# Graph attention with experts: POOL waits for the landing of its gathers in every second step

## What is computed

```python
alpha = a_src[src] + a_dst[dst]                     # leaky relu, exp(alpha - shift), then
out   = segment_sum(h[src] * coef[:, :, None], dst) # one sum per target node
```

```python
e = leaky_relu(a_src[src] + a_dst[dst]); msg = h[src] * alpha[:, :, None]
agg = segment_sum(msg, dst); scores -> top 2 of 4 -> softmax -> g
out = sum over e of g[..., e] * (gelu(x @ W1[e] + b1[e]) @ W2[e] + b2[e])
```

## Time and profile before

| | |
|---|---|
| median of the timed runs | 4169.92 us |
| profiled execution: span | 5269.4 us |
| first edge stage in it (143 to 3084 us) | 2941 us, 420 steps |
| second edge stage in it (3229 to 5126 us) | 1897 us, 265 steps |
| POOL busy | 2649.1 us, 50% of the span |
| DVE busy | 3039.4 us, 58% |
| PE busy | 3476.8 us, 66% |

### The profile page before, as it was taken

How to read it: one execution, slowest core, us unless ns; L and a number is a source line. 1 busy time by engine, 2 the same in 40 slices (tenths; PEclk the granted TensorE clock), 3 DMA queues, 4 the chain that set the end, 5 groups by cost and what they waited for, 6 DMA issues and landing times. The chain is left out here.

```text
span 5269.4 us, 87248 instructions
## 1 busy us (share of the span) xinstructions
PE 3476.8 (66%) x16727; PEld 2890.9 (55%) x16728; DVE 3039.4 (58%) x9074; ACT 1492.7 (28%) x4965; POOL 2649.1 (50%) x2767
## 2 busy tenths in 40 slices
PE   5555555665566665666655537888888888888860
PEld 4444444444454444444444436777777777777760
DVE  5566655555565666666666665555555555555558
ACT  3222222222222222222222213333333333333310
POOL 1555555555555555555555522555555555555540
PEclk9777777777777777777777766888888888888865
DMA  5322333332333333333332242111111111111118
GB/s 121 82 78 75 84 82 81 84 84 79 82 82 99 101 101 102 100 101 101 101 84 78 77 79 49 20 20 22 20 20 22 20 20 22 20 21 21 20 16 239
DMA packets 224394, 356.43 MB, mean 68 GB/s; under 512 B 65743, under 2 KB 143761, under 8 KB 224051
## 3 DMA queue, kind: packets, MB, share of 16 engines
q0 software_dynamic: 114560, 234.67, 19.2%
q1 hardware_dynamic: 100624, 109.13, 7.5%
q10 hardware_dynamic: 8867, 9.05, 0.6%
HBM read 294.17 MB, written 45.66 MB: 64 GB/s over the span
## 5 line engine op out<-in xcount | busy, mean ns | idle before, releaser
L791 POOL DMA_INDIRECT msg<-table,idx x1680 | 1630.7, 971 | 1305.1 <-ACT rel L806 844.6
L1466 POOL DMA_INDIRECT xmsg<-xtable,xidx x1060 | 1002.8, 946 | 889.0 <-ACT xidx L1482 589.7
L1159 PE MATMUL psS_e<-msg,hot 128*125 128x260 f32 x3360 | 1182.9, 513 | 281.4 <-issue 162.2
L1159 PEld LDWEIGHTS psS_e<-msg,hot 128*125 128x125 f32 x3360 | 815.5, 254 | 512.3 <-issue 337.3
L888 DVE TENSOR_TENSOR room<-room,psS_e 125x260 f32 x842 | 356.5, 423 | 361.7 <-remote 180.9
L1024 DVE TENSOR_TENSOR msg<-msg,psW_e 128x1024 f32<-128x1024 f32 x420 | 509.5, 1213 | 8.8 <-issue 1.1
L812 ACT CAST hotT<-psT_e 125x512 bf16<-125x512 f32 x422 | 244.7, 580 | 951.6 <-remote 649.7
L1012 DVE TENSOR_REDUCE look<-psD_e 128x32 f32<-128x96 f32 x420 | 106.6, 254 | 700.7 <-remote 553.8
L1076 PE MATMUL psD_e<-ad_b,hotT 125*128 x1684 | 133.9, 182 | 559.8 <-issue 151.3
L1655 PE MATMUL psY<-w,hid 128*125 128x256 f32 x1600 | 457.1, 447 | 56.7 <-issue 29.6
L1065 PEld LDWEIGHTS psT_e<-ident,hot 128*125 128x125 f32 x1692 | 320.7, 240 | 248.2 <-ACT hotT L812 157.7
(11 more groups left out here) (308 smaller groups left out, 4436.9 us busy)
## 6 DMA issues: line engine op xcount, KB each, us to landing
msg<-table,idx POOLq DMA_INDIRECT x1680
experts_out<-y_room SPq DMA_DIRECT2D x101, 224.0 KB
y_back<-experts_out SPq DMA_DIRECT2D x25, 896.0 KB
xmsg<-xtable,xidx POOLq DMA_INDIRECT x1060
xs<-x_all SPq DMA_DIRECT2D x100, 125.0 KB
table<-hrow SPq DMA_DIRECT2D x50, 113.8 KB
x_all<-in_x SPq DMA_DIRECT2D x5, 1120.0 KB
xin<-in_x SPq DMA_DIRECT2D x50, 112.0 KB
```

The lines of the kernel that those rows point to most:

```text
L791: nc.gpsimd.indirect_dma_start(msg[:, u, j, :], None, table[:, :], bass.IndirectOffsetOnAxis(ap=idx[:, u, j:j + 1], axis=0)).then_inc(gath ...
L1159: last = nc.tensor.matmul(psS[:, u % 2, j // GT, 0:ROW], hot[:, u, j, :], msg[:, u, j, :], start=j % GT == 0, stop=j % GT == GT - 1)
L1466: nc.gpsimd.indirect_dma_start(msg[:, u, j, :], None, xtable[:, :], bass.IndirectOffsetOnAxis(ap=idx[:, u, j:j + 1], axis=0)).then_inc(gat ...
```

## The change

In the first edge stage POOL, having issued the 4 gathers of step u, waits in the odd steps (u = 1, 3, 5 of the loop of 6) until the last of the 4 has landed. In the second stage it waits in the odd steps (w odd) until all 4 gathers of the step have landed. Only then does it go on to the next step's wait on `staged` and its gathers. No instruction is removed, and nothing else is changed. `gather` gets an argument for the trip, with which the awaited count is worked out.

```diff
@@ first edge stage, POOL
                             nc.gpsimd.indirect_dma_start(
                                 msg[:, u, j, :], None, table[:, :],
                                 bass.IndirectOffsetOnAxis(ap=idx[:, u, j:j + 1], axis=0)).then_inc(gathered[u][j], 16)
+                        if u % 2 == 1:
+                            pool.wait_ge(gathered[u][ST - 1], s * (TRIPS * 16) + i * 16 + 16)
@@ second edge stage, POOL
-            def gather(k, w):
+            def gather(k, w, visit):
                 u = RING[w % SPAN]
                 pool.wait_ge(staged, k + 1)
                 pool.sem_inc(opened, 1)
...
                         bass.IndirectOffsetOnAxis(ap=idx[:, u, j:j + 1], axis=0)).then_inc(gathered[u], 16)
+                if w % 2 == 1:
+                    pool.wait_ge(gathered[u], (visit * RING.count(u) + (w // XRING + 1)) * (16 * XT))
 
             with pool.Fori(0, TRIPS) as i:
                 for w in range(SPAN):
-                    gather(i * SPAN + w, w)
+                    gather(i * SPAN + w, w, i)
             for w, k in enumerate(TAIL):
-                gather(k, w)
+                gather(k, w, TRIPS)
```

## The result

The changed kernel takes 4745.23 us (median of 4 runs, 4743.74 to 4749.27) against 4171.76 us before (4 runs): 1.137 times as long, 95% interval 1.136 to 1.139. That is 573 us more. The forecast was 4719 us, 549 more.

What follows compares the result with a forecast made beforehand. The prediction took POOL's issue rate to bound the first stage and PE the second. Waits of 519 us, 10 for the loop's end and 20 for the second stage, added to 4170, gave 4719 us, range 4420 to 4860.

Steps and rivals of the forecast that it cites:

- the three floors: Phases without gathers 434 us, POOL's first-stage issues 2105, PE's second-stage busy time 1565: together 4104 us.
- 519 + 10 forecast: First stage: 210 waits at 2.47 us, paid in full, give 519 us; the loop's end adds 10 us.
- the landing: First-stage wait: the awaited gather's data lands 1.8 us after its issue ends.
- The restart of 0.81: First-stage wait: idle POOL needs 0.81 us to its next gather, 0.51 more than the usual gap of 0.30.
- The longer first issue: First-stage wait: POOL's first gather issue after a wait takes longer, 0.16 us for each wait.
- the wait at the loop's end: First stage, step u = 5: branch and counters no longer run under gather issue, 10 us over 70 trips.
- 20 forecast: Second stage: POOL stays just below the stage's time, so 132 waits of 1.9 us cost 20 us, between 0 and 251.
- B: Rival: first-stage gathers are cheaper in timed runs than in the profile; 262 us more, 4432 us; chance 0.14.
- C: Rival: timed runs have the POOL slack the profile shows, so no change, 4170 us; chance 0.08.
- D: Rival: DVE and PE code fetches meet fewer gather packets on the DMA engines; 70 us saved, 4100 us; chance 0.05.
- the contrast that I called the sharpest test: Profile after: span grows by under 200 us while the timed median grows by over 400.

Runs made afterwards that it cites:

- e0: The kernel before, unchanged, profiled once more: 4173.89 us, span 4172.0 us.
- e6: The kernel before without each first-stage step's fourth gather (tile zero, left out of the sums), no waits added: 4022.65 us, ratio 0.964.
- e9: e6 plus the change's first-stage waits in odd steps, for the third gather: 4199.62 us, 177 us over e6.
- e2: The kernel before with only the second stage's waits of the change: 4197.85 us, ratio 1.006.
- e8: The kernel before with the second stage's wait in all 265 steps, none in the first stage: 4470.56 us, ratio 1.071.
- e1: The kernel before with only the first stage's waits of the change: 4718.33 us, ratio 1.131.
- e10: e1 with the first-stage waits in steps 0, 2 and 4 of the loop instead of 1, 3 and 5: 4693.17 us, ratio 1.125.
- e3: e1 with each wait asking for the last gather of the step before, issued 5 us earlier: 4177.19 us, ratio 1.000.
- e4: e1 with each wait asking for the step's third gather instead of the fourth: 4435.72 us, ratio 1.062.
- e5: e1 with the wait for the fourth gather in every first-stage step, 420 instead of 210: 5297.85 us, ratio 1.269.

## Why the prediction was right, and where it was not

**What bounds the kernel: right, and for the first stage shown by e0, e6 and e9.** The step that carried the forecast was to add floors (phases without gathers, POOL's issue rate in the first stage, PE's busy time in the second) and find the timed median only 66 us above, instead of trusting the idle time in the trace. The second profile gives those stages as 2146 us (floor 2105) and 1585 us (I had split off 1631 and a floor of 1565).

That the sum closed so well was partly luck. PE's 1565 us came from the disturbed execution, at a granted clock of 0.83, and I had called it a floor only as long as the clock stays the same. It does not; the second stage in the second profile:

```profile
2441.70:4026.90 1585.20, 1437.80 (x8475) 1314.74 (x8476) 991.62 (x3791) 694.07 (x1415) 998.94 (x1060) 0.90 0.15 25
```

PE's own work is 1438 us there at 0.90, 91% of the stage, so 147 us of the second stage are no busy time of PE, and the three floors would have left about 190 us over instead of 66. The first stage's floor of 2105 was sound, and that is what the forecast hung on. That PE bounds the second stage stays argued from its busy share: e2 and e8 show that POOL does not, and no run takes work off PE.

**The first stage: right, 519 + 10 forecast, 556 measured by its span and 542 by e1.** By term: the landing was taken as 1.8 us behind the issue's end; it is 2.8 from its start (the median in the profile after), so 1.85. The restart of 0.81 fits: 1.85 + 0.81 = 2.66, and a gap inside the loop is 2.69. The longer first issue, 0.16 a wait, did not occur: the mean issue was 967 ns before (second profile) and is 965 after. In its place two terms were left out or small: some landings are slow (the longest is 6.3 us from its issue), and the wait at the loop's end lies 0.7 us above the others, where I had 0.15; e10 recovers 0.36 of it. The median gap inside the loop less 0.30 is 2.4, and POOL's added idle time is 2.66 a wait: that difference, 210 x 0.26 = 55 us, is what these two bring. So the total came out near by luck in part: 34 us for longer first issues (210 x 0.16), which were not there, and 10 for the loop's end stood in for these 55.

The estimate by the Trainium skill ("DMA: Bandwidth & Descriptors", "Anatomy of one DMA — SWDGE (gpsimd) path") was 2.3 us from the start; the trace after has 2.8 at the median and never under 2.7 here, so the measurement decides, and the page's price would have made the forecast 95 us lower, further off.

**The second stage: right, 20 forecast, 22 by e2 and 23 by its span.** The price of one wait is about 2.1 us, as e8 lets one work out: 7.09 - 5.0; the forecast had 1.9. It is paid only beyond the 6.0 us a step that the stage takes by itself. That 132 waits cost nearly nothing was a near thing, as the forecast had it: POOL needs 10.0 + 2.1 = 12.1 us for two steps, and the stage takes 1585 / 132.5 = 12.0 without the waits and 1609 / 132.5 = 12.1 with them. The forecast had POOL just below the stage's time (11.9 against 12.3), and it lies at it; the 20 us were a guess between two bounds, which came out right. PE's busy time in the stage also rose, from 1438 to 1449 us, so how much of the 23 us is POOL's and how much PE's isn't shown.

**The rivals.** B and C (a cheaper gather, or slack, in the timed runs) are out. The issue is 946 ns and the gap 0.30 us in an undisturbed execution too, and its span of 4172.0 us is that of the timed runs, so nothing is left that speaks for a gap only the recording has; C asked for 4170 us. D (relief for code fetches) would show as a gain with POOL at leisure. In e9, the kernel in which POOL has slack, the waits cost 177 us where POOL's own sum gives 149, so there is no sign of a gain that offsets them; no run looks at the fetches by themselves.

**What failed: the contrast that I called the sharpest test.** I forecast a span of 5270 to 5450 us for the profile after, on the step that "POOL's idle time in the first stage belongs to the profiled execution alone". I took that for a trait of *being profiled*. It belonged to one execution: the second profile of the same kernel shows neither the stops of the earlier trace rows nor the 553.8 us of the earlier trace rows, and every later profile was as long as its timed runs. What made PE and DVE stand still in the first profile isn't known; no later trace has it, and whether the timed execution of 7088 us has the same cause can't be said. The forecast of the timed median did not hang on it, that of the new profile did.

## What to carry to other kernels

When the timed median is far from the profiled span, add up each stage's floors (issue rate, busy time of the fullest engine) and see whether they reach the median; idle time in a disturbed trace is no cover for anything. Profile again before you trust the floors either, as busy times move with the clock. Where an engine issues back to back and bounds its stage, a wait for the transfer just issued costs all that is left of its landing plus the restart, every time (2.6 us here); with one issue between, half; with a step of four between, nothing. The same wait is free on an engine with slack, up to that slack and no further.

## What the runs showed of the hardware

A gather of 133 KB lands 2.8 us after its issue starts and one of 10 KB 2.4 us (medians), so thirteen times the data adds 0.4 us. An idle POOL needs 0.8 us from the landing to its next gather's record: of the median gap of 2.70 us behind a wait 1.85 are landing in the first stage of the kernel after, and of 2.28 us 1.46 are in the second stage of e8. The mean clock that PE is granted in the first stage (1 is full speed) fell with the time that POOL was held back, with the same matmuls: 0.88 in e0 and in e3, whose waits hold nothing up, 0.81 in e4, 0.78 after the change and 0.69 in e5. Here are the windows from the first gather to the last, in the second profile of before and then in the one after (the three last columns are clock, DMA share and GB/s):

```profile
146.60:2292.90 2146.30, 1523.43 (x7529) 1205.76 (x7529) 1765.33 (x4567) 709.94 (x3183) 1623.72 (x1680) 0.88 0.45 120
```

```profile
146.70:2849.10 2702.40, 1759.25 (x7541) 1371.00 (x7541) 1772.12 (x4569) 704.77 (x3187) 1620.23 (x1680) 0.78 0.36 95
```

PE's busy time rises by 236 us at 0.78 against 0.88. PE was not the bound there (6.4 us a step against 4.2 busy), so nothing of the time is put down to it. In e8 the same happens in the second stage, 0.83 against 0.90 and 1546 us busy against 1438, but with 5.8 us busy in a step of 7.09 PE was not the bound there either. Whether such pauses would cost more in a stage that PE still bounds wasn't tried.
